# Layer 1 of a four-layer kernel: key maxima as b + relu(a - b), shared by ScalarE and VectorE

## Chip, cores, metric

One Trainium2 chip, one core of it. The metric is the device time of one launch in microseconds (us), lower is better. Engines: TensorE (PE), VectorE (DVE), ScalarE (ACT), GpSimd (POOL), and SyncE (SP), which issues the DMAs.

## What is computed

Four layers, each a gated cross attention and a gated feed-forward part, over 1024 query rows x and 6404 context rows of width 128. The change is in the attention of layer 1: 16 heads of 64, keys and values from the context rows (Wm) and from the normed x itself (Wkv), 7428 keys in all.

```python
q = _split_heads(xn @ Wq)
kv = xn @ Wkv
k = _split_heads(kv[..., :INNER])
v = _split_heads(kv[..., INNER:])
mem = _split_heads(memories @ Wm)
k = jnp.concatenate([k, mem], axis=2)
v = jnp.concatenate([v, mem], axis=2)
dots = jnp.einsum('bhid,bhjd->bhij', q, k) * scale
attn = jax.nn.softmax(dots, axis=-1)
out = jnp.einsum('bhij,bhjd->bhid', attn, v)
```

## The kernel before

`l1_attention` works in 32 **units**: a head and a half of the queries (512 of them, four blocks j of 128). The softmax needs each query's maximum over all 7428 keys before its exponentials, so a unit is gone through twice. One unit ahead, the **maxima** are taken from scores in bf16: step i of `max_score` (L948) multiplies one block of 128 queries with 1024 keys, as two matmuls of 512 keys side by side on the two halves of the rows of TensorE, into the two banks of a **slot** of PSUM; `maximum` (L1146) on VectorE reduces the 1024 columns to one (L1151). A unit has 28 such steps (4 blocks x 7 chunks of 1024 keys) and two small ones for the last 260 keys, each for two blocks (L1154). There are two slots, taken in turn (`slot`, `take_slot`): a matmul of step n waits until step n-2 was read. Projections and the closing of a unit use the same slots.

Then the 59 tiles of 128 keys are **scored** in full precision (`score`, L978 and L979, in three banks in turn), ScalarE takes the exponentials (`exponential`, L1103) into a ring of ten tiles `prob` (eight of them, and two in `h`, whose memory is lent), TensorE **weighs** the values with them (`weigh`, L990), and VectorE and GpSimd sum them (**totals**: `total_up`, L1173 for tiles 0, 3 and 6 of eight, L1227 for the others). The negated maxima go through TensorE (L965) and ScalarE (`take_nm`, L1074) into row tiles of QB.

The order on every engine is written out by the same loops: a unit has 8 **rounds** r. Round r has, on TensorE, two maxima steps (part 0), the scores of eight tiles (three in round 0) with up to two **extras** behind the fourth and the sixth, two more maxima steps (part 1; none in round 0), and the weighing of the eight tiles before. The other engines walk the same loops and pick what is theirs. Maxima run 34 steps (a unit and `LEAD` = 4) ahead, done in a **prologue** before the first unit.

Extras (`extras_of`) depend on the unit within a group of four, which is a pair of heads: units 0 and 1 of a group project the next pair's queries and keys (`project` L932, `round_hi` L1054 rounds them to `hi_s` on ScalarE, `cut_lo` L1143 makes `lo_s`, the rest, on VectorE, `cast` L1214 makes `bf_s`, the bf16 keys, on GpSimd; SP stores the three to HBM); unit 2 projects nothing; unit 3 projects the values (L945, L1063). Every unit has `fin` in round 1: output projection of the unit before (L1004, L1006), from `acc`, its copy of the weighed sums (`take_acc`, L1082, two buffers). The last pair has no next pair.

KM holds a head's bf16 keys for the maxima. Its upper 64 rows have the first 512 keys of each chunk of 1024 and its lower 64 rows the second 512 (`load_max`), so the two matmuls of a step are these:

```python
for half, (j, a, k) in enumerate(step_at(i)):
    rows = slice(DH * half, DH * (half + 1))
    q = f * CH + j * P
    last = nc.tensor.matmul(c.banks(bank + half)[:, 0:k], QM[h % 2][rows, q:q + P],
                            KM[h % 2][rows, a:a + k], start=True, stop=True)
```

Of the kernel before, what the change touches and what calls it, by code (L numbers as in the profile page):

```python
# [7 lines left out]
BF16 = mybir.dt.bfloat16  # L8
# [5 lines left out]
P = 128  # L14
# [12 lines left out]
MASKED = -1e30  # L27
TWO_ONES = 1.0 + 0x3F80 / 2.0 ** 23
# [595 lines left out]
def l1_attention(c, w, scratch):  # L624
# [18 lines left out]
    LEAD = 4  # L643
    FIN_AT, NM_AT = 1, ROUNDS - 1
# [91 lines left out]

    def step_at(i):
        if i < UQ * FULL:
            return [(i // FULL, (i % FULL) * CH, CH)] * 2
        return [(2 * (i - UQ * FULL) + half, FULL * CH, REM) for half in range(2)]  # L740
# [15 lines left out]
    with ExitStack() as held:  # L756
# [14 lines left out]
        acc = sb("acc1", [P, 2, CH])  # L771
        mx = sb("mx1", [P, 2, UQ, FULL + 1])
        nm, rec = sb("nm1", [P, 2, UQ]), sb("rec1", [P, 2, UQ])
        spare = c.h[:].rearrange("p (n t) d -> p n (t d)", n=2)
# [37 lines left out]
        with phase(nc, "chain", "scored", "exped", "weighed", "slotted", "released", "v_out", "hi_out", "cast_out",  # L812
                   "totalled_d", "totalled_p", "nm_ready", "acc_out", "fin_out", "rec_ready", "added", "y_clear", "stored_0", "stored_1", "stored_2",
# [3 lines left out]
                totalled_p, nm_ready, acc_out, fin_out, rec_ready, added, y_clear, stored_0, stored_1, stored_2, weights_in_0, weights_in_1, wo_in_0,  # L817
# [99 lines left out]
            def _(pe):  # L917
# [77 lines left out]
                def finish(u):  # L995
# [6 lines left out]
                    for j in range(UQ):  # L1002
                        cols = slice(j * P, (j + 1) * P)
                        nc.tensor.matmul(c.banks(bank)[:, cols], acc[:, u % 2, cols], Wo_twice[h % 2][:],  # L1004
# [42 lines left out]
            def _(act):  # L1047
                def round_hi(k):
                    n = slot_no["k", k]
                    act.wait_ge(slotted, n + 1)  # L1050
                    if k >= DEPTH:
                        act.wait_ge(stored[k % DEPTH], stores_by(k - DEPTH))
                    m = jobs[k % JOBS][3]
# [15 lines left out]

                def take_nm(u):  # L1070
# [7 lines left out]
                def take_acc(u):  # L1078
                    act.wait_ge(weighed, ROUNDS * (u + 1))
                    if u >= 2:  # L1080
                        act.wait_ge(slotted, slot_no["fin", u - 2] + 1)
                    nc.scalar.copy(acc[:, u % 2, :], c.banks(ACC)).then_inc(acc_out, 1)  # L1082
# [31 lines left out]
                for k in range(JOBS):  # L1114
                    round_hi(k)
                    if k < GROUPS:
                        take_v(0, k)
                take_nm(0)
                for u in range(UNITS):
                    for r in range(ROUNDS):  # L1120
                        extras = extras_of(u, r)
# [15 lines left out]
            def _(dve):  # L1137
# [8 lines left out]
                def maximum(u, i):  # L1146
# [3 lines left out]
                    if i < UQ * FULL:  # L1150
                        nc.vector.tensor_reduce(mx[:, u % 2, j, i % FULL:i % FULL + 1], c.banks(slot(n), 2), AX.X,  # L1151
# [1254 lines left out]
```

## Time and profile before

| | |
|---|---|
| time, median of 3 runs | 5270.39 us (5267.61 to 5272.48) |
| profiled execution | span 5269.8 us from first to last instruction; no time of its own beside the span is given |
| TensorE matmuls, busy | 4827.1 us (92%) |
| VectorE, busy | 4327.4 us (82%) |
| ScalarE, busy | 3096.7 us (59%) |
| GpSimd, busy | 1940.9 us (37%) |
| granted TensorE clock, mean | 0.955 |

Layer 1's attention takes the span from about 330 to 2830 us. Shares over the whole span mix it with layer 0 before and layers 1 to 3 after, which the change doesn't touch; so the stretch is read by windows. Busy time of an engine is the time covered by its instructions. "Idle before" a group is time in which its engine waited just ahead of it, with the instruction that ended the wait. PEld are TensorE's weight loads. Matmuls overlap in the records: one of 512 columns is shown 0.39 us long where the next can start after 0.22.

### The profile page before, as it was taken

The page shows a single profiled execution, that of the slowest core. Times are in us where ns is not written, and L with a number is a line of the kernel's source. Part 1 is how long each engine was busy: PE and PEld are TensorE (multiplying, and loading weights), DVE is VectorE, ACT ScalarE, POOL GpSimd, SP SyncE. Part 2 cuts the span into 40 slices and gives each one's busy share as a digit, 9 for nine tenths or more (in the row PEclk, how much of TensorE's full clock was granted, in tenths as well). Part 3 has the DMA queues.
Part 4 walks back from the last instruction along what each step waited for, and adds up shares of the span by engine and source line. Part 5 has one row for each costly group of instructions (what it writes and reads, how often), then busy time and mean ns, then how long its engine had stood idle before and what let it go on. Part 6 is the DMA issues. An engine that isn't in the chain of part 4 may idle for free. (4 is left out here: it accounts for less than half of the span.)

```text
span 5269.8 us, 74714 instructions
## 1 busy us (share of the span) xinstructions
PE 4827.1 (92%) x26357; PEld 1891.5 (36%) x26366; DVE 4327.4 (82%) x4358; ACT 3096.7 (59%) x6111; POOL 1940.9 (37%) x1522
## 2 busy tenths in 40 slices
PE   8938999999999999999995699999998699999997
PEld 5623454544545454544442222222222322222222
DVE  7648878788787878878886699999996599999996
ACT  3313454454545454444442288888886288888886
POOL 0014878787787878787783100000000100000000
PEclk9968999999999999999997699999998699999998
DMA  1024334242333334142210211111110211111110
GB/s 36 5 89 117 95 92 112 60 124 51 103 81 98 98 82 122 40 123 64 51 38 15 78 29 29 29 34 29 29 23 2 78 28 29 28 29 33 30 23 6
DMA packets 171375, 298.10 MB, mean 57 GB/s; under 512 B 39061, under 2 KB 108577, under 8 KB 167393
## 3 DMA queue, kind: packets, MB, share of 16 engines
q1 hardware_dynamic: 169420, 292.95, 21.8%
q8 instruction: 213, 3.49, 0.3%
q14 instruction: 158, 1.29, 0.1%
q10 hardware_dynamic: 1584, 0.37, 0.0%
HBM read 187.39 MB, written 101.25 MB: 55 GB/s over the span
## 5 line engine op out<-in xcount | busy, mean ns | idle before, releaser
L1858 DVE TENSOR_REDUCE a_mx<-ps 128x1 f32<-128x1024 f32 x1536 | 1814.5, 1220 | 71.0 <-PE ps L1692 54.5
L1800 ACT ACTIVATE a_prob<-ps 128x512 f32<-128x512 f32 (+1 forms) x3264 | 1699.7, 601 | 288.1 <-PE ps L1680 283.3
L1227 POOL TENSOR_TENSOR tot_p<-tot_p,prob 128x512 f32<-128x512 f32 (+1 forms) x922 | 1300.4, 1410 | 401.5 <-ACT prob L1103 315.3
L1103 ACT ACTIVATE prob<-ps 128x512 f32<-128x512 f32 (+1 forms) x1512 | 801.1, 608 | 866.1 <-PE ps L979 865.2
L1151 DVE TENSOR_REDUCE mx<-ps 128x1 f32<-128x1024 f32 x896 | 1047.3, 1214 | 222.4 <-PE ps L956 222.4
L1692 PE MATMUL ps<-a_K,a_Q 59*128 59x512 bf16 (+1 forms) x3328 | 1094.7, 386 | 56.4 <-DMA a_Q<-q_stack_dram 44.5
L1680 PE MATMUL ps<-a_Q,a_K 59*128 59x512 bf16 (+1 forms) x3264 | 988.7, 383 | 55.8 <-ACT a_prob L1800 49.5
L1716 PE MATMUL ps<-a_prob,a_V 128*9 128x512 f32 x6528 | 871.8, 596 | 10.9 <-ACT a_acc L1784 10.9
L978 PE MATMUL ps<-QA,KA 128*128 128x512 f32 (+1 forms) x1888 | 841.7, 446 | 0.0
L990 PE MATMUL ps<-prob,V 128*64 128x512 f32 x3024 | 801.1, 599 | 0.7 <-ACT prob L1103 0.7
L979 PE MATMUL ps<-QB,KB 128*128 128x512 f32 (+1 forms) x1888 | 746.1, 395 | 0.0
L1173 DVE TENSOR_TENSOR tot_d<-tot_d,prob 128x512 f32<-128x512 f32 x539 | 629.3, 1167 | 134.6 <-ACT prob L1103 114.8
L1680 PEld LDWEIGHTS ps<-a_Q,a_K 59*128 59x128 bf16 (+1 forms) x3264 | 240.6, 93 | 1114.5 <-ACT a_prob L1800 920.3
L978 PEld LDWEIGHTS ps<-QA,KA 128*128 128x128 f32 (+1 forms) x1888 | 351.4, 186 | 279.0 <-ACT prob L1103 109.7
L2299 POOL MEMSET f_ones<- 128x128 f32 x1 | 0.2, 210 | 1097.5 <-POOLq L43 1097.5
L2208 POOL MEMSET f_spread<- 8x512 f32 x1 | 0.5, 515 | 1095.4 <-SPq L41 1095.4
L956 PE MATMUL ps<-KM,QM 64*128 64x512 bf16 (+1 forms) x1920 | 319.1, 383 | 69.2 <-DVE mx L1151 42.6
L979 PEld LDWEIGHTS ps<-QB,KB 128*128 128x128 f32 (+1 forms) x1888 | 354.0, 187 | 61.8 <-issue 26.8
L1692 PEld LDWEIGHTS ps<-a_K,a_Q 59*128 59x128 bf16 x3328 | 240.3, 94 | 357.5 <-DVE a_mx L1858 301.8
L990 PEld LDWEIGHTS ps<-prob,V 128*64 128x64 f32 x3024 | 224.3, 136 | 392.5 <-issue 323.6
L1227 POOL TENSOR_TENSOR tot_p<-tot_p,h 128x512 f32<-128x512 f32 x230 | 323.6, 1407 | 99.8 <-ACT h L1103 78.0
L1103 ACT ACTIVATE h<-ps 128x512 f32<-128x512 f32 (+1 forms) x376 | 212.5, 607 | 220.4 <-PE ps L979 220.3
(415 smaller groups left out, 3772.8 us busy)
## 6 DMA issues: line engine op xcount, KB each, us to landing
a_K<-k_stack_dram SPq DMA_DIRECT2D x128, 300.2 KB
k_hi_dram<-hi_s SPq DMA_DIRECT2D x112, 256.0 KB, 2.2
k_lo_dram<-lo_s SPq DMA_DIRECT2D x112, 256.0 KB, 2.4
KA<-k_hi_dram SPq DMA_DIRECT2D x64, 384.0 KB, 4.3
KA<-k_lo_dram SPq DMA_DIRECT2D x64, 384.0 KB, 5.6
KB<-k_hi_dram SPq DMA_DIRECT2D x64, 384.0 KB, 6.6
k_bf_dram<-bf_s SPq DMA_DIRECT2D x112, 128.0 KB, 1.8
KM<-k_bf_dram SPq DMA_DIRECT2D x32, 448.0 KB
```

What stands on the lines that cost most here:

```text
L978: nc.tensor.matmul(out, KA[:, cols], QA[u % 2][:], start=True, stop=False)
L979: nc.tensor.matmul(out, KB[:, cols], QB[u % 2][:], start=False, stop=True).then_inc(scored, 1)
L990: last = nc.tensor.matmul(c.banks(ACC)[DH * g:DH * (g + 1), :], V[:, t, DH * side:DH * (side + 1)], prob_of(u, t), start=(t < 2), stop=(t ...
L1103: nc.scalar.activation(prob_of(u, t)[0:r, :], c.banks(n % 3)[0:r, :], ACT.Exp, scale=SCALE).then_inc(exped, 1)
L1151: nc.vector.tensor_reduce(mx[:, u % 2, j, i % FULL:i % FULL + 1], c.banks(slot(n), 2), AX.X, ALU.max).then_inc(released, 1)
L1173: nc.vector.tensor_tensor(tot_d[0:r, u % 2, :], tot_d[0:r, u % 2, :], p, ALU.add).then_inc(totalled_d, 1)
L1227: nc.gpsimd.tensor_tensor(tot_p[0:r, u % 2, :], tot_p[0:r, u % 2, :], p, ALU.add).then_inc(totalled_p, 1)
L1680: nc.tensor.matmul(c.banks(n % 3)[0:r, :], K[(u // HALVES) % 2][0:ROWS, t * P:t * P + r], Q[u % 3][0:ROWS, :], start=True, stop=True).then ...
L1692: last = nc.tensor.matmul(c.banks(slot(step) + half)[:, 0:k], Q[u % 3][MROW:MROW + ROWS, j * P:(j + 1) * P], K[(u // HALVES) % 2][MROW:MRO ...
L1716: last = nc.tensor.matmul(c.banks(ACC)[32 * g:32 * g + VW, :], V[:, t, u // HALVES, :], prob[:, (BATCHES * u + b) % 2, g, :], start=(t < B ...
L1800: nc.scalar.activation(prob[0:r, batch % 2, t % BATCH, :], c.banks(n % 3)[0:r, :], ACT.Exp, scale=SCALE).then_inc(exped, 1)
L1858: nc.vector.tensor_reduce(mx[:, u % 2, j, i % FULL:i % FULL + 1], c.banks(slot(step), 2), AX.X, ALU.max).then_inc(maxed, 1)
```

## The change

The maximum of two numbers a and b is a + relu(b - a). In chunks 0 to 3 of 7 (`LIFTED` = 4), the second 512 keys are stored as their difference from the first 512: the product with the queries is then b - a at once. ScalarE takes its relu out of PSUM into a bf16 tile `over` (two buffers), and VectorE adds a, straight from PSUM, and takes the maximum over 512 columns, in one `tensor_tensor_reduce`. The plain steps of chunks 4 to 6 are as before. Such a step is called **raised** here; 16 of a unit's 28 full steps are.

- GpSimd's `cast` subtracts for four of the 17 projections of a pair (`differs`), and `round_hi` waits for the cast that still reads its buffer.
- The steps of a unit are put in another order (`places`): raised ones at the 14 places of part 1, ahead of a weighing, and at places 5 and 10, in part 0; the small steps at 0 and 1 instead of 28 and 29.
- `lift`, new on ScalarE, stands before a round's exponentials for part 0 and behind them for part 1.
- `acc` has one buffer instead of two, so `take_acc` waits for the `fin` of one unit ago instead of two.

```diff
+    LIFTED = 4
+    BEFORE_WEIGHING = [n for n in range(STEPS) if n % 4 < 2 and n not in (0, 1, 4, 5)] + [2, 3]
...
+    raised = [(j, s) for s in range(LIFTED) for j in range(UQ)]
+    plain = [(j, s) for s in range(LIFTED, FULL) for j in range(UQ)]
+    others = [n for n in range(STEPS) if n not in BEFORE_WEIGHING]
+    remainder = {others[0]: 0, others[1]: 2}
+    places = BEFORE_WEIGHING + others[3::3] + [n for n in others[2:] if n not in others[3::3]]
+    order = dict(zip(places, raised + plain))
+
     def step_at(i):
-        if i < UQ * FULL:
-            return [(i // FULL, (i % FULL) * CH, CH)] * 2
-        return [(2 * (i - UQ * FULL) + half, FULL * CH, REM) for half in range(2)]
+        if i in remainder:
+            return [(remainder[i] + half, FULL * CH, REM) for half in range(2)]
+        j, s = order[i]
+        return [(j, s * CH, CH)] * 2
...
+    def differs(k):
+        kind, _, a, _, _ = jobs[k % JOBS]
+        return kind == W_M and a < LIFTED * PAIR and (a // CH) % 2 == 1
...
-        acc = sb("acc1", [P, 2, CH])
+        acc = sb("acc1", [P, CH])
...
+        over = [sb(f"over{i}", [P, CH], BF16) for i in range(2)]
...
                     if k >= DEPTH:
                         act.wait_ge(stored[k % DEPTH], stores_by(k - DEPTH))
+                        if differs(k - 2):
+                            act.wait_ge(cast_out, k - 1)
...
+                def lift(u, i):
+                    if is_raised(i):
+                        n, no = slot_no["max", (u, i)], raised_no(u, i)
+                        act.wait_ge(slotted, n + 1)
+                        if no >= 2:
+                            act.wait_ge(released, freed[slot_no["max", step_of(no - 2)]][0])
+                        nc.scalar.activation(over[no % 2][:], c.banks(slot(n) + 1), ACT.Relu).then_inc(lifted, 1)
...
                 def take_acc(u):
                     act.wait_ge(weighed, ROUNDS * (u + 1))
-                    if u >= 2:
-                        act.wait_ge(slotted, slot_no["fin", u - 2] + 1)
-                    nc.scalar.copy(acc[:, u % 2, :], c.banks(ACC)).then_inc(acc_out, 1)
+                    if u >= 1:
+                        act.wait_ge(slotted, slot_no["fin", u - 1] + 1)
+                    nc.scalar.copy(acc[:], c.banks(ACC)).then_inc(acc_out, 1)
...
+                for n in range(STEPS + LEAD):
+                    lift(*divmod(n, STEPS))
                 take_nm(0)
                 for u in range(UNITS):
                     for r in range(ROUNDS):
+                        for step in max_steps(u, r, 0):
+                            lift(*step)
                         extras = extras_of(u, r)
...
+                        for step in max_steps(u, r, 1):
+                            lift(*step)
                         if r == 0 and u >= 1:
                             take_acc(u - 1)
...
-                    if i < UQ * FULL:
-                        nc.vector.tensor_reduce(mx[:, u % 2, j, i % FULL:i % FULL + 1], c.banks(slot(n), 2), AX.X,
+                    if is_raised(i):
+                        s, no = order[i][1], raised_no(u, i)
+                        dve.wait_ge(lifted, no + 1)
+                        nc.vector.tensor_tensor_reduce(out=over[no % 2][:], in0=c.banks(slot(n)), in1=over[no % 2][:],
+                                                       scale=1.0, scalar=LOWEST, op0=ALU.add, op1=ALU.max,
+                                                       accum_out=mx[:, u % 2, j, s:s + 1]).then_inc(released, 1)
+                    elif i not in remainder:
+                        s = order[i][1]
+                        nc.vector.tensor_reduce(mx[:, u % 2, j, s:s + 1], c.banks(slot(n), 2), AX.X,
                                                 ALU.max).then_inc(released, 1)
...
-                    nc.gpsimd.tensor_copy(bf_s[k % DEPTH][:, 0:m], f32(hi_s[k % DEPTH][:, 0:m])).then_inc(cast_out, 1)
+                    if differs(k):
+                        nc.gpsimd.tensor_tensor(bf_s[k % DEPTH][:, 0:m], f32(hi_s[k % DEPTH][:, 0:m]),
+                                                f32(hi_s[(k - 1) % DEPTH][:, 0:m]), ALU.subtract).then_inc(cast_out, 1)
+                    else:
+                        nc.gpsimd.tensor_copy(bf_s[k % DEPTH][:, 0:m], f32(hi_s[k % DEPTH][:, 0:m])
+                                              ).then_inc(cast_out, 1)
```

How the order moves on VectorE, in rounds 2 to 4 of a unit without projections. Before (a group of four reductions is part 1 of a round and part 0 of the next; the L1173 are the totals between them):

```order
L1151 TENSOR_REDUCE mx<-ps 128x1 x4
L1173 TENSOR_TENSOR tot_d<-tot_d,h 128x512
L1173 TENSOR_TENSOR tot_d<-tot_d,prob 128x512 x2
L1151 TENSOR_REDUCE mx<-ps 128x1 x4
L1173 TENSOR_TENSOR tot_d<-tot_d,prob 128x512
L1173 TENSOR_TENSOR tot_d<-tot_d,h 128x512
L1173 TENSOR_TENSOR tot_d<-tot_d,prob 128x512
```

The same in the change (ISA is the fused instruction and, under the same line, its second one of one column; L1202 is the plain reduction, L1224 the totals):

```order
L1197 ISA over,mx<-ps,over 128x512
L1197 ISA mx 128x1
L1197 ISA over,mx<-ps,over 128x512
L1197 ISA mx 128x1
L1202 TENSOR_REDUCE mx<-ps 128x1 x2
L1224 TENSOR_TENSOR tot_d<-tot_d,prob 128x512
L1224 TENSOR_TENSOR tot_d<-tot_d,h 128x512
L1224 TENSOR_TENSOR tot_d<-tot_d,prob 128x512
```

Of each four reductions the first two, those of part 1, became raised steps, each two instructions; the totals stand where they stood.

ScalarE in the same kind of unit, before (all exponentials):

```order
L1103 ACTIVATE prob<-ps 128x512 x4
L1103 ACTIVATE h<-ps 128x512 x2
L1103 ACTIVATE prob<-ps 128x512 x8
L1103 ACTIVATE h<-ps 128x512 x2
L1103 ACTIVATE prob<-ps 128x512 x8
```

And in the change (L1106 is `lift`, L1141 the exponentials; the first group of three is part 1 of round 1 and place 10 of round 2):

```order
L1106 ACTIVATE over<-ps 128x512 x3
L1141 ACTIVATE h<-ps 128x512 x2
L1141 ACTIVATE prob<-ps 128x512 x6
L1106 ACTIVATE over<-ps 128x512 x2
L1141 ACTIVATE prob<-ps 128x512 x2
L1141 ACTIVATE h<-ps 128x512 x2
L1141 ACTIVATE prob<-ps 128x512 x4
L1106 ACTIVATE over<-ps 128x512 x2
```

Two relus stand behind each eight exponentials, three where place 10 follows.

## Rows read from the trace of the kernel before

**Rows 1.** Windows, layer 1's attention: length, busy PE, PEld, DVE, ACT, POOL; clock, DMA

```profile
400.00:2830.00 2430.00, 2357.27 (x11112) 1163.21 (x11112) 1958.86 (x1853) 1160.92 (x2344) 1867.54 (x1400) 0.99 0.32 84
```

**Rows 2.** Windows of one unit each: with keys, and without projections

```profile
1042.30:1119.20 76.90, 75.73 (x340) 36.45 (x338) 61.16 (x63) 38.08 (x78) 60.67 (x48) 1.00 0.36 110
...
1193.70:1263.60 69.90, 67.65 (x316) 31.02 (x314) 65.14 (x54) 32.12 (x66) 55.50 (x41) 1.00 0.18 40
```

**Rows 3.** Waits over 450:2750: who for whom, us in total, times, longest

```profile
PEld ps L978 <- ACT prob L1103: 103.2, 518, 0.2
...
PE ps L956 <- DVE mx L1151: 25.5, 64, 0.5
...
PE ps L956 <- DVE lo_s L1143: 11.6, 49, 0.2
```

**Rows 4.** Timeline, a round without projections: start, length, what, count, [idle before <-releaser]

```profile
917.90 0.61 PE L956 MATMUL ps<-KM,QM 64*128 64x512 bf16 x4
...
920.41 4.60 DVE L1151 TENSOR_REDUCE mx<-ps 128x1 f32<-128x1024 f32 x4
...
922.02 0.39 PE L956 MATMUL ps<-KM,QM 64*128 64x512 bf16 x2
922.90 0.39 PE L956 MATMUL ps<-KM,QM 64*128 64x512 bf16 x2 [0.48 <-DVE mx L1151]
...
923.99 4.03 ACT L1103 ACTIVATE prob<-ps 128x512 f32<-128x512 f32 x8 [5.35 <-PE ps L979]
...
925.11 4.77 DVE L1173 TENSOR_TENSOR tot_d<-tot_d,prob 128x512 f32<-128x512 f32 x3
...
927.27 0.60 PE L956 MATMUL ps<-KM,QM 64*128 64x512 bf16 x4
```

**Rows 5.** Timeline, a round with values: last exponentials, next maxima

```profile
1000.59 1.09 ACT L1103 ACTIVATE prob<-ps 128x512 f32<-128x512 f32 x2
...
1005.04 0.61 PE L956 MATMUL ps<-KM,QM 64*128 64x512 bf16 x4
```

**Rows 6.** One line's instructions: L1151, duration ns min/median/max, first and last start

```profile
L1151 DVE TENSOR_REDUCE mx<-ps x896: 1204/1214/1227, 402.1 to 2733.4; 128x1 f32<-128x1024 f32 x180
```

**Rows 7.** Timeline, start of the prologue

```profile
401.48 1.03 PE L956 MATMUL ps<-KM,QM 64*128 64x512 bf16 x4 [14.67 <-DMA QM<-q_bf_dram]
402.13 31.76 DVE L1151 TENSOR_REDUCE mx<-ps 128x1 f32<-128x1024 f32 x28 [14.07 <-PE ps L956]
```

**Rows 8.** The instructions of L1143

```profile
L1143 DVE TENSOR_TENSOR lo_s<-ps,hi_s x136: 418/692/694, 348.0 to 2368.4; 128x512 fp32r<-128x512 f32 x128, 128x260 fp32r<-128x260 f32 x8
```

**Rows 9.** The instructions of L1180

```profile
L1180 DVE RECIPROCAL rec<-den x32: 177/178/180, 523.1 to 2818.2; 128x4 f32<-128x4 f32 x32
```

**Rows 10.** The instructions of L1063

```profile
L1063 ACT COPY V<-ps x120: 372/588/591, 349.1 to 2549.7; 128x512 f32<-128x512 f32 x112, 128x256 f32<-128x256 f32 x8
```

**Rows 11.** Timeline, a round with keys: lo_s, last exponential, maxima

```profile
856.88 0.69 DVE L1143 TENSOR_TENSOR lo_s<-ps,hi_s 128x512 fp32r<-128x512 f32 x1 [0.48 <-ACT hi_s L1054]
...
857.23 0.60 ACT L1103 ACTIVATE h<-ps 128x512 f32<-128x512 f32 x1
...
857.72 0.39 PE L956 MATMUL ps<-KM,QM 64*128 64x512 bf16 x2 [0.23 <-DVE lo_s L1143]
...
861.63 0.61 PE L956 MATMUL ps<-KM,QM 64*128 64x512 bf16 x4
```

**Rows 12.** Timeline, change of units: second step of part 0, first exponentials

```profile
889.66 0.39 PE L956 MATMUL ps<-KM,QM 64*128 64x512 bf16 x2 [0.21 <-DVE mx L1151]
...
890.64 1.55 ACT L1103 ACTIVATE prob<-ps 4x512 f32<-4x512 f32 x3 [4.13 <-PE ps L979]
```

**Rows 13.** The instructions of L1227 and L1214

```profile
L1227 POOL TENSOR_TENSOR tot_p<-tot_p,prob x922: 1249/1297/1758, 445.5 to 2811.6; 128x512 f32<-128x512 f32 x180, 4x512 f32<-4x512 f32 x5
...
L1214 POOL CAST bf_s<-hi_s x136: 392/612/1163, 348.0 to 2371.7; 128x512 bf16<-128x512 f32 x128, 128x260 bf16<-128x260 f32 x8
```

**Rows 14.** GpSimd's waits ahead of L1214: what ended them, us in total, times

```profile
  ACT hi_s L1054: 56.4, 16
```

More of the change, by code:

```diff
@@ L27 @@
 MASKED = -1e30
+LOWEST = -3.0e38
 TWO_ONES = 1.0 + 0x3F80 / 2.0 ** 23
@@ L735, in nm_no, with is_raised, raised_no, step_of @@
         return 0 if u == 0 else 1 + (TILES + 1) * (u - 1) + TILES - 1
-    def step_at(i):
-        if i < UQ * FULL:
-            return [(i // FULL, (i % FULL) * CH, CH)] * 2
-        return [(2 * (i - UQ * FULL) + half, FULL * CH, REM) for half in range(2)]
+    raised = [(j, s) for s in range(LIFTED) for j in range(UQ)]
[4 more added lines that the diff above has]
+    order = dict(zip(places, raised + plain))
+    def step_at(i):
+        if i in remainder:
+            return [(remainder[i] + half, FULL * CH, REM) for half in range(2)]
+        j, s = order[i]
+        return [(j, s * CH, CH)] * 2
+    def is_raised(i):
+        return i not in remainder and order[i][1] < LIFTED
+    RAISED = len(raised)
+    def raised_no(u, i):
+        return RAISED * u + sum(is_raised(x) for x in range(i))
+    def step_of(no):
+        u, k = divmod(no, RAISED)
+        return u, [i for i in range(STEPS) if is_raised(i)][k]
+    def differs(k):
+        kind, _, a, _, _ = jobs[k % JOBS]
+        return kind == W_M and a < LIFTED * PAIR and (a // CH) % 2 == 1
     def by_dve(t):
@@ L812, in l1_attention @@
         with phase(nc, "chain", "scored", "exped", "weighed", "slotted", "released", "v_out", "hi_out", "cast_out",
-                   "totalled_d", "totalled_p", "nm_ready", "acc_out", "fin_out", "rec_ready", "added", "y_clear", "stored_0", "stored_1", "stored_2",
+                   "totalled_d", "totalled_p", "nm_ready", "acc_out", "fin_out", "rec_ready", "added", "y_clear", "lifted", "stored_0", "stored_1", "stored_2",
                    "weights_in_0", "weights_in_1", "wo_in_0", "wo_in_1", "max_in_0", "max_in_1", "q_in_0", "q_in_1",
@@ L816, in l1_attention @@
                 block, chain, scored, exped, weighed, slotted, released, v_out, hi_out, cast_out, totalled_d,
-                totalled_p, nm_ready, acc_out, fin_out, rec_ready, added, y_clear, stored_0, stored_1, stored_2, weights_in_0, weights_in_1, wo_in_0,
+                totalled_p, nm_ready, acc_out, fin_out, rec_ready, added, y_clear, lifted, stored_0, stored_1, stored_2, weights_in_0, weights_in_1, wo_in_0,
                 wo_in_1, max_in_0, max_in_1, q_in_0, q_in_1, seg_in_0, seg_in_1, seg_in_2, seg_in_3, seg_in_4):
@@ L1003, in finish @@
                         cols = slice(j * P, (j + 1) * P)
-                        nc.tensor.matmul(c.banks(bank)[:, cols], acc[:, u % 2, cols], Wo_twice[h % 2][:],
+                        nc.tensor.matmul(c.banks(bank)[:, cols], acc[:, cols], Wo_twice[h % 2][:],
                                          start=True, stop=True)
```

## Prediction

> **What bounds the kernel now.** I read the page first. Its chain of waits covers only the last 15 us, so it says nothing of layer 1; busy times and slices do. The touched stretch is 400 to 2830 us of a 5269.8 us span. There TensorE is granted 0.99 of its clock, that is the upper level, 2.4 GHz, and is 97% busy, VectorE 81%, ScalarE 48%, GpSimd 77% [rows 1]. TensorE sets the pace, and a cheaper VectorE helps only where TensorE waits for it.
>
> The 32 units (half a head each) repeat in fours: two with projections of keys, one with none, one with values. Two windows, each one unit long [rows 2]: a first kind of 76.9 us, and the third, without projections, of 69.9. The third is the odd one: VectorE is busy 65.1 us of it, 93%, and TensorE is idle 2.2 us. The list of waits has the total over 450:2750 us [rows 3]: TensorE's maxima matmuls (L956) wait 64 times for a reduction (L1151), 25.5 us, and 49 times for lo_s (L1143), 11.6 us.
>
> One round of the third kind shows the first wait in the making [rows 4]. VectorE does four reductions in 4.60 us and three totals, one behind the other, in 4.77 (1.59 each): 9.37 us, and the round lasts 927.27 - 917.90 = 9.37 us. VectorE is full. TensorE's first step behind the weighing starts at 922.02, the second at 922.90, after a 0.48 us wait. Undisturbed, the four matmuls of two steps are a group of 0.61 us [rows 5] of which each matmul is 0.39 long, so the second step starts 0.22 behind the first. The true delay is 0.88 - 0.22 = 0.66 us, that is the idle time plus 0.18. Over 64 waits of 25.5/64 = 0.40 us mean, VectorE's maxima cost TensorE 64 x (0.40 + 0.18) = **37 us** of steady state. Without the delay this round would last 9.37 - 0.66 = 8.71 us.
>
> **The change, part by part.**
>
> *VectorE.* Of a unit's 28 full steps, 16 turn from a reduction over 1024 into a fused add and maximum over 512 and a second, one-column instruction that hands out the maximum: the order shows both. A reduction takes 1.214 us [rows 6], by spacing 1.13 to 1.18 (28 in 31.76 us [rows 7], 4 in 4.60 [rows 4]). No row has the fused instruction. Nearest is lo_s<-ps,hi_s: 128x512, one input in PSUM, one in SBUF, output in SBUF, 0.692 us median and never over 0.694 [rows 8], though GpSimd was busy around it; totals, with both inputs in SBUF, take 1.59 beside GpSimd [rows 4]. I take 0.69, as the fused one has the operands of lo_s; the other end is 1.2, two passes. The second instruction costs between nothing (swallowed by the overlap of 0.08 that the reductions show) and 0.178, the 4-column reciprocal [rows 9]; I take 0.08, half way. A raised step is then 0.77 us (0.69 to 1.4) against 1.18. The third kind's round becomes 4.77 + 2.35 + 2 x 0.77 = 8.66 us, just under TensorE's 8.71, so the 37 us go nearly whole; 3 us stay for rounds where both are tied. **-34 us.**
>
> The Trainium skill (VectorE: DVE Perf Modes, The DRAIN you can't avoid) speaks against splitting: the next Vector op does not start until the pipe of the last is empty, so keep the number of ops small. By it a raised step would be 0.692 + 0.178 = 0.87, the round 8.86, and the gain some 7 us smaller. The reductions' spacing, below their length [rows 6, 7], is against so strict a reading.
>
> *ScalarE.* It gets 512 relus of 128x512, about 0.59 each like its copies of that shape out of PSUM [rows 10]: 9.4 us a unit. 14 of a unit's 16 stand behind the round's eight exponentials, where ScalarE sits idle for 5.35 us while TensorE weighs [rows 4]: 1.2 us of relus are covered, and the weighing wants nothing from them. The other two stand ahead of a round's first exponential. At the change of units the second step's matmul starts at 889.66, behind a wait that will go, and the exponential at 890.64 [rows 12]: 0.39 for the matmul and 0.59 for the relu just fit even with that wait, and with 0.2 to spare without it. Cost 0; without the cover each of the 64 would delay one exponential by up to 0.6 us, 38 us. The order has one table load in layer 1, ahead of the exponentials, as before, so relus and exponentials don't switch tables.
>
> *The new chain, TensorE to ScalarE to VectorE to TensorE.* The two buffers `over` make ScalarE wait for the fused instruction two back, which is no later than the slot's own release. In the third kind VectorE reaches the raised steps after its totals, well behind the relus. With keys, ScalarE is through its exponentials at 857.83, with relus at 859.0, VectorE with the fused ones at 859.8; TensorE wants the slots at 861.63 [rows 11]. With values it is 1001.68, 1002.9, 1003.7, wanted at 1005.04 [rows 5]. Cost 0; at 1.4 for a raised step it would still be 0 there.
>
> *The 49 waits for lo_s* are a chain of latency: projection, hi on ScalarE, lo_s at 856.88 with VectorE idle 0.48 us before it, done 857.57, matmul 857.72 [rows 11]. A lighter VectorE doesn't shorten it: 0.
>
> *Prologue.* 34 steps at VectorE's pace, 28 in 31.76 us [rows 7]; 18 of the 34 are now raised. A raised step keeps its slot for 0.65 (matmul to VectorE: 401.48 to 402.13) + 0.6 relu + 0.77 = 2.0 us, and there are two slots: 1.0 a step instead of 1.13. Where raised and plain pairs alternate, followed, four steps take 4.3 instead of 4.5. Together 1 to 3 us: **-2 us**. At 1.4 for a raised step it would be +5.
>
> *GpSimd and SP.* Four of 17 casts per pair of heads become subtractions, 32 in all, about 1.3 us like its totals, instead of 0.61 [rows 13]. 28 lie in steady state, at most one in a round: +19 us of GpSimd, which is busy 60.7 of 76.9 us there [rows 2] and for which L956 and the scores don't wait [rows 3]. SP issues that bf16 store 0.7 us later and with it the next hi store; the staging buffer comes round three projections, over a round, later. ScalarE's new wait (hi_s k for the cast of k-2) is met in the prologue, since GpSimd is idle there ahead of 16 casts, 56.4 us in all [rows 14]: even if half of it lay ahead of the first, nearly 2 us each. Cost 0; without cover 0.7 x 28 = 20 us.
>
> *acc* with one buffer waits for the fin of one unit ago, read most of a unit earlier: 0. The small steps (260 keys) fall in another round: same matmuls, 0.
>
> Sum: -34 - 2 = **-36 us** from the profiled execution's span of 5269.8, which is 0.6 below the median of the three runs: **5234 us** (-0.7%).
>
> The Trainium skill (Vector Engine (DVE) Microarchitecture Reference, Measured stream behaviour on trn2) gives built-in and multi-uOp programs the same 1.0417 ns a column and about 75 ns. An estimate from it is 0.61 us for the fused instruction; the sum would be -39, with nothing kept back for ties. The reductions agree, 1.14 by it and 1.13 in [rows 7].
>
> **Rivals.**
> - *A, as forecast*, 5225 to 5246: one end has the 37 whole, the prologue at 3 and 5 more from rounds whose lateness hides below the list; the other leaves 0.25 us in each of 50 rounds.
> - *B, the fused instruction isn't short* (slower). It decides in the third kind: 4.77 + 2.35 + 2r equals today's 9.37 at r = 1.13. At r = 1.4 it is 9.92, +0.55 us in 55 rounds, +30, prologue +5: 5305. For: no row shows it, it is a program of its own. Against: 512 columns, and lo_s's operands.
> - *C, it meets GpSimd* as totals do, r about 1.1: no steady gain, prologue +2: 5268 to 5274. Against: lo_s never rose over 0.694 [rows 8].
> - *D, relus delay exponentials.* Scores already wait for ScalarE, 518 times 0.2 us [rows 3]. If the 64 relus ahead of scores cost 0.3 to 0.6 each, 20 to 38 us go back: 5254 to 5272. Against: the timetable above. The Trainium skill (ScalarE: Activation LUTs, Rules for kernel authors) puts relu on VectorE, not ScalarE; here that is the engine with 7% left instead of the one idle half the time.
> - *E, the delay moves to another releaser*, GpSimd's totals or ScalarE: 5260 to 5268. Against: VectorE at 93% in the third kind alone.
>
> **Numbers.** About 0.2% (10 us) is what a measurement here can tell from no change. A 0.74, B 0.09, C 0.04, D 0.09, E 0.04. The range takes A with 3 us below, and D and E up to 5264: 0.8. Faster (below 5260) is A and half of D, 0.79; the same is C, E and the rest of D, 0.12; slower is B, 0.09.
>
> **What would show it.** Right: units of the third kind 66.5 to 67.5 us, the others 0 to 0.8 shorter; in 450:2750 waits of L956's matmuls for maxima under 5 us, for lo_s still about 11; the fused instruction 0.6 to 0.7 us, VectorE's busy time down by 150 to 230 us, ScalarE's up by 300 and its gap ahead of a round's exponentials near 3.5 us in the third kind, GpSimd's up by 20. Wrong: a fused instruction over 1.1 (B, C); longer waits of the scores for exponentials in rounds that open with a relu (D); a new releaser ahead of L956 or L978 (E).

## The result, and the profile after

| | before | the change |
|---|---|---|
| time, median | 5271.43 us (5267.61 to 5277.61, 4 runs) | **5229.37 us** (5228.63 to 5230.47, 4 runs) |
| ratio | | 0.9921, 95% [0.9907, 0.9935] |
| span of the profiled execution | 5269.8 us | 5227.6 us (its own time 5229.35) |
| granted TensorE clock, mean | 0.955 | 0.955 |

The change is faster by 42 us, 0.8%, four times what a measurement here can tell from no change. The forecast was 5234 in a range of 5222 to 5264. Lines moved: L956 is now L984 (maxima matmuls), L979 is L1007 (scores), L990 L1018 (weighing), L1103 L1141 (exponentials), L1151 L1202 (plain reduction), L1143 L1187 (lo_s). New are L1106 (`lift`'s relu), L1197 (the fused instruction, which the trace calls CUSTOM_DVE_ANT_0) and L1266 (`cast`'s subtraction).

The page of the change: busy time, share and count of each engine, then three of its costliest groups (busy, mean ns | idle time ahead and who ended most of it):

```profile
PE 4813.3 (92%) x26366; PEld 1882.8 (36%) x26366; DVE 4069.5 (78%) x4870; ACT 3357.1 (64%) x6623; POOL 1961.0 (38%) x1522
...
L1202 DVE TENSOR_REDUCE mx<-ps 128x1 f32<-128x1024 f32 x384 | 455.2, 1220 | 271.5 <-PE ps L984 271.5
...
L1197 DVE CUSTOM_DVE_ANT_0 over<-ps,over 128x512 bf16<-128x512 f32 x512 | 334.8, 685 | 111.1 <-ACT over L1106 110.2
...
L1106 ACT ACTIVATE over<-ps 128x512 bf16<-128x512 f32 x512 | 287.5, 621 | 191.3 <-PE ps L984 190.5
```

The fused instruction is 0.685 us long and adds 334.8/512 = 0.65 of busy time, since two in a row overlap; its second instruction, which hands out the maximum (the **read-out**, DVE_READ_ACCUMULATOR2_ANT below), adds almost nothing. A plain reduction takes 455.2/384 = 1.19. VectorE lost 4327.4 - 4069.5 = 258 us, ScalarE gained 260, GpSimd 20. The same instructions by line show how steady they are (min/median/max in ns):

```profile
L1197 DVE CUSTOM_DVE_ANT_0 over<-ps,over x512: 676/685/693, 403.5 to 2696.5; 128x512 bf16<-128x512 f32 x171
...
L1197 DVE DVE_READ_ACCUMULATOR2_ANT mx<- x512: 75/82/86, 404.1 to 2697.1; 128x1 f32 x171
...
L1106 ACT ACTIVATE over<-ps x512: 592/619/669, 402.7 to 2694.5; 128x512 bf16<-128x512 f32 x171
...
L1266 POOL TENSOR_TENSOR bf_s<-hi_s x32: 1255/1273/1817, 360.4 to 2317.8; 128x512 bf16<-128x512 f32 x32
```

The windows that answer to [rows 1, 2]: the whole stretch, a unit with keys, the third kind (without projections), and one with values. Columns as there.

```profile
400.00:2830.00 2430.00, 2356.71 (x11161) 1163.31 (x11161) 1729.41 (x2404) 1430.53 (x2872) 1885.28 (x1400) 0.98 0.32 84
...
1030.70:1107.20 76.50, 75.54 (x340) 36.32 (x340) 54.25 (x79) 46.19 (x93) 61.71 (x48) 1.00 0.37 113
1181.20:1247.90 66.70, 66.70 (x316) 30.40 (x316) 55.58 (x70) 40.24 (x82) 55.60 (x41) 1.00 0.19 41
1247.90:1326.40 78.50, 78.50 (x428) 44.81 (x428) 46.05 (x70) 48.54 (x96) 57.36 (x42) 1.00 0.30 70
```

The third kind fell from 69.9 to 66.7 us, and TensorE is busy in it from end to end, at the same granted clock of 1.00. VectorE's share there is 83%, from 93.

The waits over 450:2750, against [rows 3]. No row has L984 waiting for a maximum any more:

```profile
PEld ps L1006 <- ACT prob L1141: 106.3, 535, 0.2
...
DVE over L1197 <- ACT over L1106: 102.9, 112, 2.6
...
PE ps L984 <- DVE lo_s L1187: 11.7, 49, 0.2
```

VectorE now waits 102.9 us for relus, but in rounds in which TensorE wants nothing from it yet. A round of the third kind, the counterpart of [rows 4]:

```profile
1196.08 0.61 PE L984 MATMUL ps<-KM,QM 64*128 64x512 bf16 x4
1196.68 1.13 ACT L1106 ACTIVATE over<-ps 128x512 bf16<-128x512 f32 x2
...
1198.64 0.68 DVE L1197 CUSTOM_DVE_ANT_0 over<-ps,over 128x512 bf16<-128x512 f32 x1
1199.25 0.08 DVE L1197 DVE_READ_ACCUMULATOR2_ANT mx<- 128x1 f32 x1
1199.25 0.68 DVE L1197 CUSTOM_DVE_ANT_0 over<-ps,over 128x512 bf16<-128x512 f32 x1
...
1200.20 0.61 PE L984 MATMUL ps<-KM,QM 64*128 64x512 bf16 x4
1200.63 2.36 DVE L1202 TENSOR_REDUCE mx<-ps 128x1 f32<-128x1024 f32 x2 [0.70 <-PE ps L984]
1201.51 1.09 ACT L1141 ACTIVATE h<-ps 128x512 f32<-128x512 f32 x2 [3.70 <-PE ps L1007]
...
1204.83 0.61 PE L984 MATMUL ps<-KM,QM 64*128 64x512 bf16 x4
```

Round: 1204.83 - 1196.08 = 8.75 us instead of 9.37. Both pairs of maxima steps are undisturbed groups of 0.61 now, and the idle time has changed sides: VectorE waits 0.70 us for the matmuls. The two fused instructions start 0.61 apart, and the read-out lies wholly inside the next one. The relus follow the matmul and are over before VectorE is through with its totals.

**Where the 42.2 us of span went.** Measured from copy of `acc` to copy of `acc`, the four kinds of a group of units were 74.5, 69.95, 78.9 and 76.9 us and are 73.96, 66.68, 78.55 and 76.51. (The first, the one that [rows 2] does not show, is the other with keys.) So: third kind 7 x 3.28 = 22.9; 7 x 0.55 = 3.9; values 7 x 0.33 = 2.3; 6 x 0.39 = 2.3; the last three units, which have no next pair to project, 9.0. That is 40.4 of steady state. So not all of it lies where VectorE is full: 8.5 us (3.9 + 2.3 + 2.3) come from units with keys and values, mostly at the change of units, where the second maxima step was about 0.38 us late before. The prologue, from its first maxima matmul to the first score, took 39.15 us and takes 37.6: 1.5. It starts 0.65 earlier, the first unit is 0.6 shorter, and the rest of the program is 1.0 longer.

### The profile page after: what moved, and what is told of

The parts are those of the page before. It is cut to its first block and busy times, and to the rows that moved or that the text cites. A ratio compares the mean times of both kernels' runs of the same rounds, so it can differ in the third digit from the quotient of the medians.

```text
span 5227.6 us, 76770 instructions
## 1 busy us (share of the span) xinstructions
PE 4813.3 (92%) x26366; PEld 1882.8 (36%) x26366; DVE 4069.5 (78%) x4870; ACT 3357.1 (64%) x6623; POOL 1961.0 (38%) x1522
## 5 line engine op out<-in xcount | busy, mean ns | idle before, releaser
L1748 PE MATMUL ps<-a_K,a_Q 59*128 59x512 bf16 (+1 forms) x3328 | 1094.7, 386 | 56.6 <-DMA a_Q<-q_stack_dram 44.7
L1141 ACT ACTIVATE prob<-ps 128x512 f32<-128x512 f32 (+1 forms) x1512 | 801.4, 609 | 511.7 <-PE ps L1007 510.7
L1018 PE MATMUL ps<-prob,V 128*64 128x512 f32 x3024 | 801.1, 599 | 0.7 <-ACT prob L1141 0.7
L1007 PE MATMUL ps<-QB,KB 128*128 128x512 f32 (+1 forms) x1888 | 746.6, 395 | 0.0
L1224 DVE TENSOR_TENSOR tot_d<-tot_d,prob 128x512 f32<-128x512 f32 x539 | 619.4, 1149 | 146.0 <-ACT prob L1141 129.5
L1202 DVE TENSOR_REDUCE mx<-ps 128x1 f32<-128x1024 f32 x384 | 455.2, 1220 | 271.5 <-PE ps L984 271.5
L1197 DVE CUSTOM_DVE_ANT_0 over<-ps,over 128x512 bf16<-128x512 f32 x512 | 334.8, 685 | 111.1 <-ACT over L1106 110.2
L1106 ACT ACTIVATE over<-ps 128x512 bf16<-128x512 f32 x512 | 287.5, 621 | 191.3 <-PE ps L984 190.5
L1007 PEld LDWEIGHTS ps<-QB,KB 128*128 128x128 f32 (+1 forms) x1888 | 354.0, 188 | 62.0 <-issue 26.8
L1018 PEld LDWEIGHTS ps<-prob,V 128*64 128x64 f32 x3024 | 224.3, 136 | 397.7 <-issue 323.7
L1283 POOL TENSOR_TENSOR tot_p<-tot_p,h 128x512 f32<-128x512 f32 x230 | 325.7, 1416 | 88.4 <-ACT h L1141 66.6
```

Source lines behind the costliest of these rows:

```text
L1007: nc.tensor.matmul(out, KB[:, cols], QB[u % 2][:], start=False, stop=True).then_inc(scored, 1)
L1018: last = nc.tensor.matmul(c.banks(ACC)[DH * g:DH * (g + 1), :], V[:, t, DH * side:DH * (side + 1)], prob_of(u, t), start=(t < 2), stop=(t ...
L1141: nc.scalar.activation(prob_of(u, t)[0:r, :], c.banks(n % 3)[0:r, :], ACT.Exp, scale=SCALE).then_inc(exped, 1)
L1202: nc.vector.tensor_reduce(mx[:, u % 2, j, s:s + 1], c.banks(slot(n), 2), AX.X, ALU.max).then_inc(released, 1)
L1224: nc.vector.tensor_tensor(tot_d[0:r, u % 2, :], tot_d[0:r, u % 2, :], p, ALU.add).then_inc(totalled_d, 1)
L1283: nc.gpsimd.tensor_tensor(tot_p[0:r, u % 2, :], tot_p[0:r, u % 2, :], p, ALU.add).then_inc(totalled_p, 1)
```

## The experiments

Ten kernels were run. The kernel before was timed beside each group of them (5272.67 to 5272.88 us).

| run | median us | ratio, 95% | third kind |
|---|---|---|---|
| new order alone | 5284.15 (9 runs) | 1.0022 [1.0013, 1.0032] | 70.7 |
| two chunks raised | 5260.34 (10) | 0.9976 [0.9967, 0.9986] | 68.5 |
| six chunks raised | 5243.83 (4) | 0.9947 [0.9932, 0.9962] | 67.2 |
| before, half of each reduction | 5221.60 (4) | 0.9900 [0.9884, 0.9917] | 66.6 |
| fused step made as dear as a reduction | 5319.08 (4) | 1.0090 [1.0075, 1.0105] | 71.9 |
| relus ahead of a weighing done twice | 5252.76 (5) | 0.9964 [0.9950, 0.9978] | 67.3 |
| the change, extras a slot earlier | **5206.62** (4) | 0.9876 [0.9862, 0.9891] | 66.7 |
| before, extras a slot earlier | 5248.36 (4) | 0.9954 [0.9939, 0.9969] | 69.8 |
| three chunks, extras a slot earlier | 5218.45 (4) | 0.9894 [0.9877, 0.9910] | 67.1 |
| the change with plain casts | 5227.24 (4) | 0.9914 [0.9899, 0.9928] | 66.7 |

### The order alone

```diff
-    LIFTED = 4
+    LIFTED = 0
```

> The change with no chunk raised: the new order of steps (small ones at places 0 and 1), one acc buffer, all 28 full steps plain reductions, no relu, no subtraction. Theory (the gain is VectorE's shorter work in units where it was full): nothing is gained; units of the third kind stay at 69.5 to 70.5 us, L956-type waits for maxima about 25 us in 450:2750, time 5265 to 5275. Rival (the gain came from the order of the steps): third kind 67 us, time 5229 to 5240.

Measured: 5284.15 us, 11 above before. That the order is worth nothing was wrong: it costs. The two small steps, cheap for VectorE, stood ahead of the weighing of round 6 and stand in part 0 of round 7 now, so that one more pair of full reductions meets a weighing in every unit. (The run has the one `acc` buffer of the change too.) The waits of this run, and its window of a third kind:

```profile
PE ps L984 <- DVE mx L1202: 35.0, 80, 0.6
```

```profile
1199.90:1270.60 70.70, 67.85 (x316) 31.13 (x314) 65.44 (x54) 32.09 (x66) 55.50 (x41) 1.00 0.18 40
```

80 waits instead of 64. The 16 more all stand in part 0 of round 7, 0.65 to 0.69 us late each, in units of the third kind and in the shorter unit with keys, which is 75.3 us long instead of 74.5; the other two kinds are as before. Against this kernel, its own order, the raising of four chunks gains 5284.2 - 5229.4 = 55 us; 11 of those pay the order back.

### Two and six chunks raised

```diff
-    LIFTED = 4
+    LIFTED = 2
```

> Two chunks raised instead of four: 8 raised steps a unit, in part 1 of rounds 1 to 4; rounds 5 to 7 are plain. Theory (what counts is VectorE's work in each round of its own): in the third kind the delays of rounds 1 to 4 go, those behind rounds 5, 6 and 7 stay, some 0.65 us each, so a unit of the third kind is 68.4 to 69.2 us, and the time 5244 to 5258. Rival (VectorE's mean share over a unit counts, and half the relief already gives it slack): 66.7 us and 5229 to 5236.

```diff
-    LIFTED = 4
+    LIFTED = 6
```

> Six chunks of seven raised, 24 of 28 steps, so that 10 relus a unit stand ahead of scores, four times two in one round. Theory (VectorE has nothing left to give and the relus are free only where ScalarE idles): behind two relus the first exponential starts 0.2 to 0.3 us late, in 4 rounds of each of 31 units, and TensorE's scores with it: 5240 to 5257. Rival (relus are free wherever they stand, and VectorE's time still counts): 5222 to 5231.

With two chunks the third kind is 68.5 us, inside the expected 68.4 to 69.2, and the waits for maxima are down to 19.6 us, from the 35.0 of the order alone:

```profile
PE ps L984 <- DVE mx L1202: 19.6, 49, 0.6
```

What is left stands behind rounds 5 to 7, where the steps are still plain. The time, 5260.34, is 2 us above the range: the order's cost was not in it, and shows in the shorter unit with keys, 75.1 us.

Six chunks gave 5243.83 us, inside the expected range and 14 worse than four. VectorE is lighter still, 53.23 us of a third kind, and the unit is 0.5 longer (its window, then the start of a round that opens with two relus):

```profile
1184.40:1251.60 67.20, 67.18 (x316) 30.42 (x316) 53.23 (x78) 44.09 (x91) 55.67 (x41) 1.00 0.20 41
```

```profile
1194.98 0.61 PE L984 MATMUL ps<-KM,QM 64*128 64x512 bf16 x4
1195.41 1.09 ACT L1106 ACTIVATE over<-ps 128x512 bf16<-128x512 f32 x2 [2.83 <-PE ps L984]
...
1196.38 4.04 ACT L1141 ACTIVATE prob<-ps 128x512 f32<-128x512 f32 x8
...
1199.67 0.60 PE L984 MATMUL ps<-KM,QM 64*128 64x512 bf16 x4
```

Compare a round of the change that opens with one relu (it ends with the maxima at 1196.08, shown above):

```profile
1191.50 0.60 PE L984 MATMUL ps<-KM,QM 64*128 64x512 bf16 x4
1191.93 0.60 ACT L1106 ACTIVATE over<-ps 128x512 bf16<-128x512 f32 x1 [2.81 <-PE ps L984]
...
1192.80 4.03 ACT L1141 ACTIVATE prob<-ps 128x512 f32<-128x512 f32 x8 [0.27 <-PE ps L1007]
```

One relu leaves 0.27 us to spare. Two don't fit: the first exponential starts right behind them, 1.40 us behind the first maxima matmul (1196.38 - 1194.98; with one relu 1192.80 - 1191.50 = 1.30), and the scores that wait for its bank are late by as much. The next maxima come after 1199.67 - 1194.98 = 4.69 us instead of 1196.08 - 1191.50 = 4.58. In the unit of the window rounds 2 and 3 lose 0.11 us each in this way; round 1, which also opens with two relus and has `fin` in it, is 10.68 us long instead of 10.40; round 0 loses nothing. Together that is the unit's half microsecond. So the delay was expected too large (0.2 to 0.3) in two rounds and is absent in one. That is rival D, at the size of one relu more.

### Half of each reduction left out

```diff
-                        nc.vector.tensor_reduce(mx[:, u % 2, j, i % FULL:i % FULL + 1], c.banks(slot(n), 2), AX.X,
+                        nc.vector.tensor_reduce(mx[:, u % 2, j, i % FULL:i % FULL + 1], c.banks(slot(n)), AX.X,
```

On the kernel before: each full step reduces the first 512 of its 1024 columns, and the maxima of the other 512 keys are left out. No relu, no order, no differences.

> The kernel before, with each full reduction over the first 512 of its 1024 columns; the maxima of the other 512 keys are left out, no relus. VectorE's step is then 0.69 us as in the change, without ScalarE in it. Theory (the relus cost TensorE nothing in steady state): units as in the change within 0.1 us, 66.7 for the third kind, 76.5, 73.95 and 78.55 for the others; only the prologue is shorter, 34 steps at 0.67 us and not at 1.1, some 14 us: 5212 to 5218. Rival (relus ahead of or behind the exponentials take something back): units shorter than the change's by 0.3 us or more, time under 5208.

Measured: 5221.60 us, 3.6 above the expected range, and units of 73.96, 66.7, 78.56 and 76.48 us. Its windows of the third kind and of one with keys, then its reduction by line:

```profile
1170.90:1237.50 66.60, 66.60 (x316) 30.36 (x314) 51.69 (x54) 32.07 (x66) 55.52 (x41) 1.00 0.19 41
...
1020.40:1096.90 76.50, 75.55 (x340) 36.35 (x341) 48.49 (x63) 38.10 (x78) 60.69 (x48) 1.00 0.37 113
```

```profile
L1151 DVE TENSOR_REDUCE mx<-ps x896: 671/681/693, 403.2 to 2679.4; 128x1 f32<-128x512 f32 x180
```

This run says most. VectorE does 3.9 us less per unit than in the change (51.69 against 55.58), ScalarE does no relu at all, and every kind of unit is equal to the change's within 0.05 us. So in steady state the change has all that a lighter VectorE can give, and its relus, its longer chain, its one `acc` and its subtractions cost nothing there. The two kernels differ in the prologue, 26.6 us against 37.6: 11 us, where 14 were expected. What the edit doesn't touch took part of it back in this run: the maxima start 1.7 us later, and what follows layer 1's attention is 3.2 us longer.

### The fused step made as dear as a reduction

```diff
+        extra_mx = sb("extra_mx", [P, 2])
...
+                        nc.vector.tensor_reduce(extra_mx[:, no % 2:no % 2 + 1], c.banks(slot(n)), AX.X, ALU.max)
                         nc.vector.tensor_tensor_reduce(out=over[no % 2][:], in0=c.banks(slot(n)), in1=over[no % 2][:],
```

The change, with a reduction over 512 columns, used by nobody, ahead of each fused instruction.

> The change with a reduction over 512 columns put ahead of every fused instruction, its result unused, so that a raised step costs VectorE about 1.26 us by spacing, a little more than the 1.18 of a plain one. Theory (VectorE's time per step is all that the change won): everything is given back and the third kind lasts 70.5 to 72 us, the others 75 to 76 and 77 to 79, time 5285 to 5310. Rival (the earlier release by its place counts too): under 5270.

Its instructions by line, the waits for them, and the window of a third kind:

```profile
L1199 DVE CUSTOM_DVE_ANT_0 over<-ps,over x512: 670/680/682, 403.6 to 2786.1; 128x512 bf16<-128x512 f32 x171
...
L1198 DVE TENSOR_REDUCE extra_mx<-ps x512: 674/686/693, 403.0 to 2785.5; 128x1 f32<-128x512 f32 x171
```

```profile
PE ps L985 <- DVE mx L1199: 51.2, 85, 1.2
```

```profile
1210.00:1281.90 71.90, 67.89 (x316) 31.15 (x316) 65.92 (x86) 40.23 (x82) 55.60 (x41) 1.00 0.18 39
```

By spacing a raised step takes VectorE 1.21 us now. The time is 5319.08 us, 46 above before (11 of them the order's) and 9 above the expected range. All four kinds are longer (75.8, 71.9, 79.5, 78.1), the prologue takes 44.7. The gain is the shortness of the fused instruction and nothing else; had it been two passes, rival B would have come true, and dearer than the prediction priced it.

### Relus ahead of a weighing done twice

```diff
...
+                        if i in BEFORE_WEIGHING:
+                            doubled_by[0] += 1
+                            nc.scalar.activation(over[no % 2][:], c.banks(slot(n) + 1), ACT.Relu).then_inc(doubled, 1)
+                            act.wait_ge(doubled, doubled_by[0])
                         nc.scalar.activation(over[no % 2][:], c.banks(slot(n) + 1), ACT.Relu).then_inc(lifted, 1)
```

> The change with every relu behind the exponentials done twice, one after the other, so that ScalarE has 14 more a unit, 8.5 to 9 us. Theory (they lie in ScalarE's idle time while TensorE weighs, 3.5 us or more a round are left): units stay within 0.1 us, only the prologue is 3 to 8 us longer: 5232 to 5238. Rival (the chain of relu, fused instruction and slot is already tight): units with keys or values longer by 1 us or more, 5250 or above.

(`doubled` is a semaphore; ScalarE waits for the first relu before it starts the second.) Measured: 5252.76 us, 15 above the range. In 12 of the 14 places the second relu cost nothing, as expected. The other two, places 2 and 3, lie in part 1 of round 7, the last of a unit, where ScalarE first makes the row tiles of negated maxima (`take_nm`, 1.1 us). There the doubled relus (L1110, L1112) reach TensorE, and each unit is 0.6 longer (third kind 67.3):

```profile
1255.20 0.60 ACT L1112 ACTIVATE over<-ps 128x512 bf16<-128x512 f32 x1
...
1255.94 0.69 DVE L1203 CUSTOM_DVE_ANT_0 over<-ps,over 128x512 bf16<-128x512 f32 x1 [0.42 <-ACT over L1112]
1256.78 0.39 PE L984 MATMUL ps<-KM,QM 64*128 64x512 bf16 x2 [0.41 <-DVE mx L1203]
```

Its list of waits over layer 1 has them all:

```profile
PE ps L984 <- DVE mx L1203: 12.3, 30, 0.4
```

30 waits of 0.41 us, each 0.6 late by spacing: 18 us; the prologue, which is a chain through ScalarE, takes 43.6 instead of 37.6, 6 us more. 18 + 6 = 24, and 5252.8 - 5229.4 = 23. The same spot in the change (its L1112 is `take_nm`):

```profile
1240.25 1.10 ACT L1112 ACTIVATE QB<-ps,ident 4x128 fp32r<-4x128 f32 x4
1241.38 1.08 ACT L1106 ACTIVATE over<-ps 128x512 bf16<-128x512 f32 x2
...
1242.74 0.69 DVE L1197 CUSTOM_DVE_ANT_0 over<-ps,over 128x512 bf16<-128x512 f32 x1
1243.35 0.08 DVE L1197 DVE_READ_ACCUMULATOR2_ANT mx<- 128x1 f32 x1
...
1243.91 0.61 PE L984 MATMUL ps<-KM,QM 64*128 64x512 bf16 x4
```

The second fused instruction hands over at 1243.35. The second step's matmul comes 0.22 behind the first, at 1244.13, and a hand-over takes 0.23 (in the run above, 1256.55 to 1256.78): 0.55 us to spare. Two relus more, 1.2 us, less 0.55 is the 0.6 that was seen. So the cover of the relus holds in all places of the change, and is thinnest ahead of the change of units, where it is 0.55 us, about one relu.

### Extras a slot earlier, on the change and on the kernel before

```diff
-    EXTRAS_BEHIND = (3, 5)
+    EXTRAS_BEHIND = (2, 4)
```

> The change, with the extras behind the third and fifth score of a round instead of the fourth and sixth. Theory (the 49 waits for lo_s are latency of projection, hi and lo_s, and are what is left of slot waits): the slot is free 0.4 us earlier than wanted, the waits vanish with 49 x (0.23 + 0.18) = 20 us: 5207 to 5213. Rival (the wait moves to the first extra, which now comes sooner behind the part 0 steps, or to the scores): 5222 to 5232.

> The kernel before with nothing but the extras moved one score earlier. Theory (the waits for lo_s and those for maxima are separate losses): its 49 waits for lo_s go, 20 to 23 us, the 64 for maxima stay: 5249 to 5253, third kind still 69.9 us. Rival (without the change VectorE is too late with lo_s, or the maxima wait more): 5258 or above.

The 49 waits for lo_s were left over. With the projections one score earlier, lo_s is done when the maxima want its slot. The change so edited, timeline of a round with keys, and a window of the unit of [rows 2]:

```profile
842.78 0.69 DVE L1187 TENSOR_TENSOR lo_s<-ps,hi_s 128x512 fp32r<-128x512 f32 x1
843.46 0.60 PE L984 MATMUL ps<-KM,QM 64*128 64x512 bf16 x4
```

```profile
1024.10:1098.90 74.80, 74.80 (x340) 36.69 (x338) 54.62 (x79) 46.19 (x93) 62.59 (x48) 1.00 0.38 115
```

No wait for lo_s is left in the list; the two kinds with keys fell from 73.96 to 72.65 and from 76.51 to 74.83 us, and the time to 5206.62 us, 1.2% below before. On the kernel before the same edit gives 5248.36, 24 less, and leaves the other loss as it was (its waits over layer 1):

```profile
PE ps L956 <- DVE mx L1151: 25.1, 63, 0.5
```

Both are a little better than expected: 0.4 us below 5207 and 0.6 below 5249. The two losses are independent: 24 and 42 apart, 66 together.

### Three chunks with extras earlier

```diff
-    LIFTED = 4
+    LIFTED = 3
...
-    EXTRAS_BEHIND = (3, 5)
+    EXTRAS_BEHIND = (2, 4)
```

> The change with the extras one score earlier and three chunks raised instead of four: 12 raised steps a unit, in part 1 of rounds 1 to 6, none in round 7, none ahead of scores. Theory (each round whose part 1 is plain delays the next part 0 where VectorE is late): against the version with four chunks and early extras, 5206.6, a delay of 0.5 to 0.7 us comes back at most changes of units: 5217 to 5227. Rival (with lo_s out of the way three chunks are enough, and fewer relus help): 5200 to 5209.

Measured: 5218.45 us, as expected, 12 above four chunks. Units are 73.0, 67.1, 78.6 and 75.2 us, each 0.1 to 0.4 longer, and maxima are late again at the changes of units, 23 times by the list, 4.7 us of waits in all. Four chunks beat two and six without this edit, and three with it.

### The change with plain casts

```diff
-                    if differs(k):
+                    if False:
```

The 32 subtractions become casts as before; the differences are left out, and the maxima are of other numbers.

> The change with plain casts instead of the 32 subtractions on GpSimd; the difference of the key chunks is left out, so the raised steps take a + relu(b). Theory (GpSimd's 20 us more are hidden): 5227 to 5231, the change's own time. Rival (they delay totals or the stores of keys): 5215 to 5225.

Measured: 5227.24 us (5225.39 to 5229.90) against 5229.37: some 2 us for the 20 that GpSimd works more, and that is no more than the runs spread; the four kinds of units are the change's within 0.02 us. As expected.

## Why the prediction was right

**What bounds the kernel** stood: TensorE, delayed by VectorE's maxima. The half reductions show it best, since they touch VectorE alone and bring the same units. The loss is wider than the third kind, though, by whose rounds the prediction reckoned its ties and rival B. In the trace of before, 41 of the 64 waits stand inside units without projections (the third kind and the last three), 0.63 to 0.71 us late each, and 23 at changes of units, where VectorE is not full on the mean, about 0.38 late. The sum took all 64 at their mean and so had both.

**Steady state, -34.** Measured: -40.4, with -0.6 for the first unit and +1.0 behind layer 1. The price of a delay was right: of the 64 listed waits the prediction made 37.1 us, and the spacing of the matmuls, second step's start less first step's less 0.22, summed in the trace of before over all pairs, gives 36.4 for them and 3.5 more in 23 pairs whose lateness, 0.14 to 0.18 each, is too small for the list. The step that was mis-sized is "3 us stay for rounds where both are tied". It stood on 8.66 against 8.71 us, a near tie; the raised step was cheaper, 0.61 by spacing instead of 0.77, and nothing stayed. (The 0.77 put a length, 0.69, where a spacing belonged, though the reductions had shown the two to differ by 0.08.) So 3 us too little were taken, and the 3.5 below the list, which the range had as one end of A, belonged in the sum.

**The fused instruction**, 0.69 taken, is 0.685, never over 0.693. "One input in PSUM, one in SBUF" was the right neighbour, and GpSimd beside it doesn't slow it. The read-out, "half way" between 0 and 0.178, is 0.082 long and costs nothing where the next fused instruction or reduction follows at once, as it lies inside that one. VectorE's busy time fell by 258 us, more than the 150 to 230 named as a sign, because of the cheaper step. The sentence of the Trainium skill (VectorE: DVE Perf Modes, The DRAIN you can't avoid) that the prediction used, by which the next Vector op waits for an empty pipe, is not borne out here: starts at 1198.64 and 1199.25 are 0.61 apart at a length of 0.685. The same section adds, and the prediction left out, that a next op that is not held starts earlier; with that the trace agrees. The 0.61 that the prediction estimated from the Trainium skill (Vector Engine (DVE) Microarchitecture Reference, Measured stream behaviour on trn2) is what the trace has, though the page measured that rate on built-in ops and the trace calls this one custom.

**ScalarE, cost 0.** Right: the gap ahead of a round's exponentials is 3.70 us (forecast 3.5), the scores' waits went from 103.2 to 106.3 us, and the units equal those of a kernel without any relu. ScalarE's busy time grew by 260 us instead of 300, though the relus' lengths add up to 318: in the records a relu overlaps with the relu behind it (1.13 us for both) and with exponentials next to it. The timetable "just fit" was right too, but its margin was looked for in the wrong place. The prediction watched the exponential behind a relu; the doubled relus show that a tight spot is places 2 and 3 in round 7, behind `take_nm`. The advice of the Trainium skill (ScalarE: Activation LUTs, Rules for kernel authors) to keep relu on VectorE would by all signs have cost the gain. No run put them there, but the fused step made as dear as a reduction gives VectorE about that much more work, and is 46 us slower than before; on ScalarE the 512 relus take no time outside the prologue, as the half reductions show.

**The new chain, cost 0.** Right for the change. "At 1.4 for a raised step it would still be 0 there" looked at rounds inside units, and misses the changes of units: with a raised step of 1.21 the second step of round 0 is about 0.60 us late at every change of units (before: 0.38 at three of four), and units with keys grew to 75.8 and 78.1, those with values to 79.5. Rival B was therefore priced too low. It counted third-kind rounds alone, by which 1.21 would be 55 x 0.17 = 9 us of steady state; measured were 46 in all, of which the order is 11 and the prologue 5.6. The 0.17 itself was right: late pairs inside the third kind went from a mean of 0.68 us to 0.84.

**The order, "0".** Right for the change and wrong in itself: alone it costs 11 us. With raised steps VectorE has the room and the cost is gone, as the half reductions in the old order show, whose units are the same.

**Prologue, -2.** Measured -1.5 (-2.2 with its earlier start). The working left out two handoffs, 0.37 us, and had the fused instruction 0.16 too long. Two slots turn over in 2.23 us in this chain, 1.12 a step and not 1.0:

```profile
408.36 0.61 PE L984 MATMUL ps<-KM,QM 64*128 64x512 bf16 x2 [0.58 <-DVE mx L1202]
...
409.01 0.60 ACT L1106 ACTIVATE over<-ps 128x512 bf16<-128x512 f32 x1 [2.83 <-PE ps L984]
...
409.75 0.69 DVE L1197 CUSTOM_DVE_ANT_0 over<-ps,over 128x512 bf16<-128x512 f32 x1 [0.40 <-ACT over L1106]
...
410.59 0.61 PE L984 MATMUL ps<-KM,QM 64*128 64x512 bf16 x2 [0.49 <-DVE mx L1197]
```

From the relu's end (409.61) to the fused instruction are 0.14 us, and from that instruction's hand-over (0.61 behind its start) to the matmul 0.23.

**lo_s, 0.** Right: 11.6 us became 11.7. **GpSimd and SP, 0.** Right within the spread of the runs, by the one with plain casts.

**Rivals.** B, C: the fused instruction is short, beside GpSimd too. D: not with one relu; it sets in with two (six chunks), at 0.11 to 0.28 us. E: no new releaser ahead of L984; the third kind has TensorE busy from end to end.

## What to carry to other kernels

Work that is moved from a full engine to an idle one is worth no more than the delays of the bounding engine that the full one causes: price those by the spacing of that engine's instructions, since the list of waits leaves out both part of each and the smallest ones. Before building the clever version, leave the suspected work out of the old kernel (here half of each reduction): that gives the ceiling of the idea in one run. And where an engine's gaps are to hold new work, look for the spot where it already has something else to do, because the margin there and not the mean decides how much fits.

## What the hardware showed that was not expected

- The instruction that hands out an accumulated maximum (one column, 0.082 us) takes no time of VectorE's own where a fused instruction follows at once: 217 such pairs, each with a read-out between, start 0.61 us apart (at most 0.617), as do the bare 512-column reductions of the run with half reductions (0.607).
- Fusing the add with the maximum costs nothing: 0.685 us for add and maximum of 512 columns from PSUM and SBUF, with a bf16 output of 512 columns, against 0.681 for a bare maximum of as many (the run with half reductions).
- The fused instruction, with one input in SBUF, isn't slowed by GpSimd: it took 676 to 693 ns in all 512 cases, in 310 of which GpSimd was busy for 90% or more of its length. Totals, with both inputs in SBUF, took 0.68 to 1.60 us in the same kernel; that GpSimd is what stretches them is not shown here.
